# First attention with two float32r parts per operand, paired scores on two halves of the array, and expert folding moved into the images

## The reference

```python
normed = normed * gn_w[None, :, None] + gn_b[None, :, None]
qkv = jnp.einsum('oc,bct->bot', qkv_w, normed) + qkv_b[None, :, None]
q, k, v = jnp.split(qkv, 3, axis=1)
...
q = (q * scale).reshape(b * N_HEADS, ch, t)
k = (k * scale).reshape(b * N_HEADS, ch, t)
...
weight = jnp.einsum('bct,bcs->bts', q, k)
weight = jax.nn.softmax(weight.astype(jnp.float32), axis=-1).astype(q.dtype)
a = jnp.einsum('bts,bcs->bct', weight, v).reshape(b, c, t)
out = jnp.einsum('oc,bct->bot', proj_w, xf + a) + proj_b[None, :, None]
...
h = jnp.einsum('td,edh->teh', xf, w1) + b1[None]
gated = jax.nn.silu(jnp.einsum('teh,ehf->tef', h, wg) + bg[None]) * (jnp.einsum('teh,ehf->tef', h, wv) + bv[None])
```

## Time and profile before

| what | us |
|---|---|
| median of 3 runs (2272.18 to 2274.57) | 2273.43 |
| the profiled execution, and its span | 2275.42, 2273.5 |
| TensorE busy in the span | 1929.1 (85%) |
| VectorE busy | 1436.2 (63%) |
| ScalarE busy | 1098.7 (48%) |
| maxima on VectorE (line 779, 1,024 of them) | 639.7 |
| exponentials on ScalarE (line 726, 512) | 497.4 |
| maxima on TensorE (line 550, 1,024) | 358.6 |
| scores on TensorE (line 652, 1,024) | 308.2 |
| PV on TensorE (line 632, 2,048 records) | 272.8 |

### The profile page before, as it was taken

The page is one execution under the profiler, slowest core; times in us unless marked ns, Lnnn a source line. Parts: engine busy times, 40 slices in busy tenths (PEclk is TensorE's granted clock), DMA queues, the critical chain, the costliest instruction groups (busy, mean ns, idle before and its releaser), DMA issues. The chain is left out here.

```text
span 2273.5 us, 41046 instructions
## 1 busy us (share of the span) xinstructions
PE 1929.1 (85%) x13306; PEld 1073.3 (47%) x13307; DVE 1436.2 (63%) x3154; ACT 1098.7 (48%) x1682; POOL 755.4 (33%) x883
## 2 busy tenths in 40 slices
PE   5769999999999999998589996996659992699993
PEld 2331223332332323232367774554447661599992
DVE  4769888888888888871346665762235665344444
ACT  4550665666666666666144442541225551344442
POOL 0232003343333333345335553000001667355551
PEclk9875999999999999999699998999879996799995
DMA  3851532323232323012333333322100242233326
GB/s 127 193 217 33 78 55 29 60 35 65 31 66 29 66 29 66 2 38 63 105 86 99 95 99 119 111 84 61 38 29 29 62 136 81 71 94 92 90 72 229
DMA packets 134782, 180.00 MB, mean 79 GB/s; under 512 B 44592, under 2 KB 87856, under 8 KB 132336
## 3 DMA queue, kind: packets, MB, share of 16 engines
q1 hardware_dynamic: 116208, 138.25, 25.6%
q0 software_dynamic: 18432, 39.88, 5.2%
HBM read 99.04 MB, written 69.01 MB: 74 GB/s over the span
## 5 line engine op out<-in xcount | busy, mean ns | idle before, releaser
L779 DVE TENSOR_REDUCE mx<-bank 128x1 f32<-128x512 f32 x1024 | 639.7, 696 | 86.4 <-PE bank L550 85.2
L726 ACT ACTIVATE P<-bank 128x1024 f32<-128x1024 f32 x512 | 497.4, 1021 | 313.1 <-PE bank L652 312.9
L550 PE MATMUL bank<-ks,qs 96*128 96x512 bf16 x1024 | 358.6, 402 | 35.5 <-DVE mx L779 35.5
L1290 POOL DMA_INDIRECT results<-yo,places x284 | 274.1, 965 | 283.6 <-DVE yo L1280 236.8
L652 PE MATMUL bank<-qs,ks 99*128 99x512 bf16 x1024 | 308.2, 384 | 2.6 <-ACT P L726 1.8
L1206 PE MATMUL bank<-xt,up 128*128 128x256 f32 x1136 | 274.8, 386 | 3.7 <-DVE xt L1257 1.4
L632 PE MATMUL bank<-P,vt 128*32 128x512 f32 x2048 | 272.8, 605 | 0.7 <-ACT P L726 0.7
L2289 POOL DMA_INDIRECT dispatched<-planes,places x128 | 124.5, 973 | 420.2 <-DVE stats L2133 357.3
L1206 PEld LDWEIGHTS bank<-xt,up 128*128 128x128 f32 x1136 | 207.5, 193 | 30.4 <-issue 4.7
L550 PEld LDWEIGHTS bank<-ks,qs 96*128 96x128 bf16 x1024 | 99.8, 98 | 257.5 <-DVE mx L779 177.7
L652 PEld LDWEIGHTS bank<-qs,ks 99*128 99x128 bf16 x1024 | 78.0, 97 | 280.0 <-ACT P L726 182.8
(11 more groups left out here) (298 smaller groups left out, 2581.8 us busy)
## 6 DMA issues: line engine op xcount, KB each, us to landing
xr<-dispatched SPq DMA_DIRECT2D x142, 130.0 KB
qk_parts<-parts SPq DMA_DIRECT2D x16, 768.0 KB, 5.1
qs<-qk_parts SPq DMA_DIRECT2D x84, 128.0 KB
ks<-qk_parts SPq DMA_DIRECT2D x84, 128.0 KB
v_turned<-vt SPq DMA_DIRECT2D x8, 1024.0 KB, 5.6
vt<-v_turned SPq DMA_DIRECT2D x8, 1024.0 KB
bands<-results SPq DMA_DIRECT2D x32, 256.0 KB, 3.7
y<-results SPq DMA_DIRECT2D x32, 256.0 KB
```

Source lines behind the costliest of these rows:

```text
L550: pe.matmul(bank[:, slot, :], qs[par][0:KB, h, c * C:(c + 1) * C], ks[par][0:KB, h, half * HALF:(half + 1) * HALF], start=True, stop=True) ...
L726: act.activation(P[:, x % SLOTS, :], bank[:, 2 * pair:2 * pair + 2, :] .rearrange("p a t -> p (a t)"), ACT.Exp).then_inc(probs_ready, 1)
L779: dve.tensor_reduce(mx[:, k // 2, k % 2:k % 2 + 1], bank[:, slot, :], AX.X, ALU.max).then_inc(unit_freed, 1)
L1290: pool.indirect_dma_start(yd_dram, bass.IndirectOffsetOnAxis(places[:, p, q:q + 1], 0), yo[:, p, q, :], None).then_inc(sent[p], 16)
```

## The change

q and k are split into two float32r parts (fp32 storage, rounded on writing) instead of three bf16 parts, by one copy on ScalarE and one subtraction. Three products of parts make 48 rows, and two rows carry the maxima. Heads go in pairs: the first head of a pair has rows 0 to 63 of the stacks, the second rows 64 to 127 (`stack_rows`), so the two scores of a pair use different rows of the array. Maxima come in twos of one head (the two halves of k), and `order_of_heads` puts the score of the same head last ahead of them, so that maxima follow a score on the same rows.

The folding goes into the bodies: one expert in each of images 1 to 6, two in image 7, as three units each (`fold_turn`, `fold`, `fold_bias`) in the same three banks. VectorE now copies the results out. The source has its own buffer, and SP loads it behind the second projection unit of each body. `STEP_OF` deals the maxima out in twos, each two counted as one.

```diff
-Q_PARTS = (0, 0, 0, 1, 1, 2)
-K_PARTS = (0, 1, 2, 0, 1, 0)
+Q_PARTS = (0, 0, 1)
+K_PARTS = (0, 1, 0)
 KB = len(Q_PARTS) * CH
-KM = KB + 3
+KM = KB + 2
+PAIRS = HEADS // 2
+ROWS = C // 2
...
+def stack_rows(u, r):
+    return slice(u * ROWS + r * CH, u * ROWS + (r + 1) * CH)
...
-    parts = sb("parts", [C, 2, 2, 3, T], BF16)
+    parts = sb("parts", [C, 2, 2, 2, T], F32)
...
-                if db is not None:
-                    for s, rest_ready in enumerate((q_rest, k_rest)):
-                        act.wait_ge(rest_ready, db + 1)
-                        act.activation(parts[:, 1 - p, s, 1], rest[:, s], ACT.Copy).then_inc(second_parts, 1)
...
-                        act.activation(parts[:, p, s, 0], qk[:, s], ACT.Copy).then_inc(first_parts, 1)
+                        act.activation(parts[:, p, s, 0].bitcast(F32R), qk[:, s], ACT.Copy).then_inc(first_parts, 1)
...
+        def split(eng, s, b, p, ready):
+
             eng.wait_ge(first_parts, b * 2 + s + 1)
-            eng.tensor_tensor(rest[:, s], qk[:, s], parts[:, p, s, 0], ALU.subtract).then_inc(rest_ready, 1)
-
-        def split_last(eng, s, b, p, split):
-
-            eng.wait_ge(second_parts, b * 2 + s + 1)
-            eng.tensor_tensor(parts[:, p, s, 2], rest[:, s], parts[:, p, s, 1], ALU.subtract).then_inc(split, 1)
+            eng.tensor_tensor(parts[:, p, s, 1].bitcast(F32R), qk[:, s], parts[:, p, s, 0], ALU.subtract).then_inc(ready, 1)
...
+            for u in range(2):
+                pool.memset(stacks0[1][u * ROWS + 32:(u + 1) * ROWS], 1.0).then_inc(ones_set, 1)
+                pool.wait_ge(ones_set, u + 1)
...
+    for step, k in ((11, 0), (21, 1)):
+        for n, kind in enumerate(("fold_turn", "fold", "fold_bias")):
+            at = (step + 2 * n) * len(units) // STEPS
...
+BODY_GROUPS = [unit for unit in BODY_UNITS if unit[0] != "max" or unit[1] % 2 == 0]
+STEP_OF = {unit: index * STEPS // len(BODY_GROUPS) for index, unit in enumerate(BODY_GROUPS)}
+STEP_OF.update({("max", k): STEP_OF["max", k - 1] for k in range(1, MAXIMA, 2)})
...
+def order_of_heads(now):
+
+    u = next((maximum(k)[2] for _, (kind, k) in now if kind == "max"), 1)
+    return 1 - u, u
...
-                for part in range(3):
-                    sp.dma_start(qs[par][KB + part:KB + part + 1, 4 * g:4 * g + 4, :]
-                                 .rearrange("p h (c t) -> p (h c) t", t=C),
-                                 nm_parts[:, part, :]).then_inc(rows_loaded, 16)
+                for u in range(2):
+                    for part in range(2):
+                        row = u * ROWS + KB + part
+                        sp.dma_start(qs[par][row:row + 1, 2 * g:2 * g + 2, :].rearrange("p h (c t) -> p (h c) t", t=C),
+                                     nm_parts[16 * u:16 * u + 16, part, :]).then_inc(rows_loaded, 16)
...
+            def load_source(e, unit, base, units):
+                sp.wait_ge(unit_filled, base + units.index(unit) + 1)
+                sp.dma_start(wres[:, e, 0:2 * C], to_fold[e, :, 0:W1_COLS]).then_inc(source_loaded, 16)
+                sp.dma_start(source[:], to_fold[e, :, W1_COLS:W1_COLS + WGV_COLS + 2]).then_inc(source_loaded, 16)
...
-                        for u in range(2):
-                            head = 4 * g + 2 * pair + u
-                            ins = pe.matmul(bank[:, 2 * pair + u, :], ks[par][:, head, s * C:(s + 1) * C],
-                                            qs[par][:, head, n * HALF:(n + 1) * HALF], start=True, stop=True)
+                        behind = now[:first_half(now)] if pair == 0 else now[first_half(now):]
+                        for u in order_of_heads(behind):
+                            rows_of = slice(u * ROWS, u * ROWS + KM)
+                            ins = pe.matmul(bank[:, 2 * pair + u, :], ks[par][rows_of, 2 * g + pair, s * C:(s + 1) * C].bitcast(F32R),
+                                            qs[par][rows_of, 2 * g + pair, n * HALF:(n + 1) * HALF].bitcast(F32R), start=True, stop=True)
...
+            def copy_product(e, slot, filled):
+                dve.wait_ge(unit_filled, filled)
+                dve.tensor_copy(wres[:, e, 0:4 * C], bank[:, slot, :]).then_inc(unit_freed, 1)
```

More of the change, by code:

```diff
@@ L334, in units_of_a_body, with expert_of, maximum, first_half @@
     units[94:94] = [("ranks", 0)]
+    for step, k in ((11, 0), (21, 1)):
+        for n, kind in enumerate(("fold_turn", "fold", "fold_bias")):
+            at = (step + 2 * n) * len(units) // STEPS
+            while units[at][0] == "max" and units[at][1] % 2:
+                at += 1
+            units.insert(at, (kind, k))
     return units
 LEAD, MAXIMA = 80, 2 * HEADS * TC
+FOLDS = ("fold_turn", "fold", "fold_bias")
 BODY_UNITS = units_of_a_body()
-STEP_OF = {unit: index * STEPS // len(BODY_UNITS) for index, unit in enumerate(BODY_UNITS)}
+BODY_GROUPS = [unit for unit in BODY_UNITS if unit[0] != "max" or unit[1] % 2 == 0]
+STEP_OF = {unit: index * STEPS // len(BODY_GROUPS) for index, unit in enumerate(BODY_GROUPS)}
+STEP_OF.update({("max", k): STEP_OF["max", k - 1] for k in range(1, MAXIMA, 2)})
+def expert_of(before, k):
+    return before + k if before == B - 2 else before
+def maximum(k):
+    pair, c, u, half = k // 32, k // 4 % TC, k // 2 % 2, k % 2
+    return pair, c, u, half
+def order_of_heads(now):
+    u = next((maximum(k)[2] for _, (kind, k) in now if kind == "max"), 1)
+    return 1 - u, u
+def first_half(now):
+    return 2 if now and now[0][1][0] == "max" else 1
 def of_next(unit):
@@ L347, in units_of @@
 def units_of(prev, more):
-    return [unit for unit in BODY_UNITS if (more or not of_next(unit)) and (prev or unit[0] in ("max", "rows"))]
+    return [unit for unit in BODY_UNITS if (more or not of_next(unit)) and (prev or unit[0] in ("max", "rows"))
+            and not (unit[0] in FOLDS and unit[1] == 0 and more)]
 FIRST_UNITS = [unit for unit in units_of(False, True) if of_next(unit)]
@@ L545, in take_max @@
             def take_max(b, par, k, slot):
-                h, c, half = k // 16, k // 2 % TC, k % 2
+                pair, c, u, half = maximum(k)
+                rows = slice(u * ROWS, u * ROWS + KB)
                 if k % 64 == 0:
                     pe.wait_ge(qk_loaded[k // 64], b * LOADS)
-                pe.matmul(bank[:, slot, :], qs[par][0:KB, h, c * C:(c + 1) * C],
-                          ks[par][0:KB, h, half * HALF:(half + 1) * HALF], start=True, stop=True).then_inc(unit_filled, 1)
+                pe.matmul(bank[:, slot, :], qs[par][rows, pair, c * C:(c + 1) * C].bitcast(F32R),
+                          ks[par][rows, pair, half * HALF:(half + 1) * HALF].bitcast(F32R), start=True, stop=True).then_inc(unit_filled, 1)
             def project(b, n, slot):
@@ L778, in reduce @@
                 dve.wait_ge(unit_filled, filled)
-                dve.tensor_reduce(mx[:, k // 2, k % 2:k % 2 + 1], bank[:, slot, :], AX.X, ALU.max).then_inc(unit_freed, 1)
+                pair, c, u, half = maximum(k)
+                row = 32 * (pair // 2) + 16 * u + 8 * (pair % 2) + c
+                dve.tensor_reduce(mx[:, row, half:half + 1], bank[:, slot, :], AX.X, ALU.max).then_inc(unit_freed, 1)
                 if k % 64 == 63:
```

213 lines of the change are left out of this document (83 added, 130 removed).

## The result

The changed kernel takes **2409.09 us** (median of four runs, 2391.88 to 2424.99), the kernel before 2272.8 beside it: 1.0597 times as long, 95% interval 1.0510 to 1.0684. I had predicted 2239, at most 2300. The profiled execution took 2419.76. Its four runs go by the clock: 2391.88 at a mean granted clock of 0.860, 2424.99 at 0.836.

What follows compares the result with a forecast made beforehand. The bound was taken to be a ring of waits between VectorE and TensorE, neither engine alone. From 2275.4 us, -14 -2 -4 -2 +2 -15 = -35 gave 2240.4, less 2.0 for the median: 2239 us; own range 2218 to 2262, wider 2218 to 2300.

Steps and rivals of the forecast that it cites:

- The failed step: Attention, TensorE's clock: stays full in image 7 despite half-microsecond gaps per step, so no fall expected in the other images.
- the uneven table: Attention steps with maxima in twos: 16 of four at 2.71 us, 8 of six at 3.89, the rest two or none.
- the fold: Experts' folding moved into images 1 to 7: 4.4 us per expert in a middle image, between 2.3 and 5.9.
- The ring: Attention's chain of waits between VectorE and TensorE: a step of four maxima goes from 2.93 to 2.71 us.
- I take 0.22: Score pair in attention: each matmul takes 0.22 us, and the pair together 0.22 instead of 0.44.
- the rival of fp32's rate: Attention: float32r matmuls take 0.43 us, TensorE bounds, period near 130, whole kernel 2410; chance 0.12.
- my rival of bare weight loads: Attention: the first maximum's load is no longer hidden under the score, ring grows by 0.11 us, 2267; chance 0.08.
- Pair in series: Attention: a pair's two scores run one after the other, 0.22 us returns per step, 56 in all, 2295; chance 0.10.
- First stage and start: First stage with one split pass less, -14 us; start of attention with a shorter first VectorE copy, -2.
- The tail: After attention: blank-row batches follow each other without source loads between, -15 us, bounded at some 20 by POOL's sends.
- six places of 0.3: Middle image: VectorE has run dry where four or six maxima follow two or none; 0.3 us each, 1.7 added.
- 4.2 less 2.6 for image 7: Image 7: two folds half covered, +4.2 us, less 12 x 0.22 = 2.6 from the pairs, about +2.

Runs made afterwards that it cites:

- `f32r_tail`: `halves_tail` with its parts in float32r instead of bf16, units still dealt evenly and the folding in the tail: 2275.62 us.
- `series`: The changed kernel with both scores of a pair on the same 50 rows, so that they run one behind the other: 2701.37 us.
- `bf16_even`: The changed kernel with bf16 parts and its units dealt evenly, four or five a step; folding stays in the images: 2259.61 us.
- `halves_tail`: The kernel before with q and k split in two bf16 parts, each head on 48 rows, pairs at once, even dealing, folding in the tail: 2206.48 us.
- `full_rows`: The changed kernel with both heads of a pair stacked, every score and maximum over both (98 and 96 rows, float32r), scores in series: 2369.25 us.
- `padded`: The changed kernel with bf16 parts and q stacks padded with zeros to 96 rows, so that a pair's scores run in series: 2287.30 us.
- `max48`: The kernel before with one line changed, its maxima taken over 48 of the 96 rows: 2332.75 us.

## Why the prediction was wrong, point by point

- **The failed step** is the sentence "The granted clock stays full in that image with these gaps, so I expect no fall of it in the others." The gaps of the last image are of a kernel on 96 rows, which also kept its clock through 2.56 of 4 us. On 48 rows the clock fell to 1.2 GHz behind stretches of 2.26, and also behind fuller ones (3.48 of 4 us), it stayed low for longer, and the uneven table and the fold made more of the falls. The size: at full clock one half of an image took 58.82, the other would by `f32r_tail` (50.07), the fold (5.3) and the table (0.7) take some 56; six such images and one without fold (104.8, as the first period of `f32r_tail`) make an estimated 794 for 930.63. The falls in these images are some 137 us. The other 42 by which they grew (794 for 752) are the weight load, the fold and the table at full clock, and the start and the tail gave back 45. The Trainium skill, page TensorE: Matmul & The Clock Gate, section A second HAM failure mode: psum-queue depth-cycling, describes a kernel whose clock goes to and fro because TensorE idles for short times between groups of matmuls. The fall behind 2.26 of 4 us agrees; `series`, with records filling 1162 of 1173 us, goes beyond it.
- **The ring** was right in every link for bf16 and wrong for the operands that the change has. "I take 0.22" held for the float32r matmul's rate, and the rival of fp32's rate fell. That its price, 2410, and its sign, a period near 130, came all the same (2409.09; 133 in the mean of the seven) is chance. But I priced the matmul and not its weight load: 0.11 in front of PV and 0.12 in front of the first maximum. That is the mechanism of my rival of bare weight loads, with float32r's longer load as its cause instead of the rows; at 5.0 us an image or more (108.23 for at most 103.24) it takes at least 40 us. The Trainium skill, same page, section Weight-path perf modes — Fast Weight Load (FWL) and DoubleRow, names a faster weight load for 128 columns unless the type is fp32; the rows 0.09 and 0.18 agree, if float32r counts as fp32 there.
- **Pair in series** did not come: in bf16 the first maximum follows the start of its pair by 0.22 (214.38 to 214.60), one matmul's time.
- **The uneven table** was priced as about neutral, and at full clock it is (0.7 in half an image); a step of six took 4.14 (844.45 to 848.59), which is the 2.95 and twice 0.59. That it makes the clock fall I didn't price.
- **The fold** at 4.4 an image measured 5.3 in its half and 4.9 in the image at full clock; the direction and the place were right.
- **First stage and start**: -16 predicted, -24.2 measured. The q/k projection of image 7 started at 127.40 for 145.22, so seven steps gave 17.8 and not 14; VectorE's first copy took 3.46 for 6.88.
- **The tail**: -15 predicted, -20.7 measured; the mechanism held. All 15 DMAs of blank rows go in one chain, and SP's first DMA of the experts follows it. POOL's last row send starts at 1285.56, as the chain's last issue ends, so the gain reached the bound of some 20 that I had named:

```profile
1261.34 24.18 SPq L511 DMA_DIRECT2D dispatched<-a  x15
1291.49 0.60 SPq L1164 DMA_DIRECT2D rec<-biases  x1
```

- Three small slips in the sum change nothing: six places of 0.3 make 1.8 and not 1.7, 4.2 less 2.6 for image 7 is 1.6, and 2240.4 less 2.0 is 2238.4.
- With a full clock in the seven images the profiled execution would have taken about 2419.76 - 137 = 2283, where the kernel before took 2275.42: the weight loads and the fold ate the gains even so. In bf16 with even steps the change gives 2206.48 with the folding left in the tail, or 2259.61 with the folding in the images.

## What to carry to other kernels

A change that takes work off the bounding engine also takes away what keeps its clock up: look at the narrowest stretch of TensorE in the trace (here 2.56 of 4 us in the routing's steps), and ask what will be left of it after the change, in time and in rows. Price a new operand type by its weight load as well as its matmul, at each place where the load is not covered. And move work into a loop only if the loop has a gap for it: what was 4 us in the tail cost 5.3 in its half of an image at full clock, and with the falls some 10 (the halves with fold in `bf16_even` take 60.7 in the mean, in `halves_tail` 50.1).

## What the runs showed of the hardware

- With scores and maxima on 48 to 50 rows, one behind the other, and records in 99% of the time, TensorE ran at 1.2 GHz for most of 1173 us (`series`); with the same on 96 to 98 rows it had 2.4 GHz for nearly all of 875 (`full_rows`). The values of these two runs differ. With rows of zeros for half of the 96 to 98 the clock was 0.98 (`padded`, bf16).
- A float32r matmul of 512 columns takes about as long as a bf16 one (maxima start 0.23 us apart, 851.10 and 851.33 in the changed kernel, for 0.22); its weight load of 128 columns takes 0.18 for 0.09.
- A load of 96 rows starts 0.23 us after a pair of 99-row scores, under it; a load of 48 rows behind the same pair starts 0.53 after it (`max48`), and the image is 5.1 us longer. Why is not shown. Behind a pair on 50 rows a 48-row load starts 0.11 after it (850.76 to 850.87 in the changed kernel).
- Not settled: why the same half rows hold 0.80 in the changed kernel (0.95 in `f32r_tail`, with even steps and no fold in the images) and only 0.60 in `series`, where two scores stand behind each other instead of beside each other and the records leave less idle time.
